# A two-layer gated cross-attention network: a new order of units in each attention's opening and in its rows, and the second attention's code without a loop

## The chip, the cores and the metric

One core of a Trainium2 chip runs the whole network in one launch. The metric is the time of that launch on the device in microseconds (us), less is better. Times come from three runs; the trace comes from one further execution that the hardware profiler recorded.

## The reference

`x` is 8 rows of 224 x 512, the context 8 rows of 750 x 512, both float32. Layer 0 has 16 heads of 32 and an unmasked softmax, layer 1 has 8 heads of 64 and a mask. Four stages follow one another, each gated by a tanh:

```python
x = x + jnp.tanh(g_xattn[0]) * _L0_xattn_ref(_layernorm(x, axis=-1), ctx_1024, ctx_1024, Wq, Wk, Wv, Wo)
x = x + jnp.tanh(g_ffn[0]) * _L0_ffn_ref(_layernorm(x, axis=-1), w1, conv_w, conv_b, w2)
x = x + jnp.tanh(g_xattn[1]) * _L1_xattn_ref(_layernorm(x, axis=-1), ctx_1024, mask, Wq, Wkv, Wo)
x = x + jnp.tanh(g_ffn[1]) * _L1_ffn_ref(_layernorm(x, axis=-1), w_gate, w_up, w_down)
...
    attn = jnp.einsum('bhnd,bhmd->bhnm', q, k) * SCALE        # attention: q from x, k and v from the context
    attn = jax.nn.softmax(jnp.where(mask[:, None, :, :], attn, -jnp.inf), axis=-1)
    out = jnp.einsum('bhnm,bhmd->bhnd', attn, v)
    return out.transpose(0, 2, 1, 3).reshape(B, N, C) @ Wo
```

The first feed-forward block quantises its weights to -1, 0, 1 and has a depthwise convolution; the second rounds activations and weights to FP4 in blocks of 16.

## The kernel before

The stages run one behind another and share the names of their buffers (`a_` is an attention, `f_` a feed-forward block). Both attentions are one function, called twice; `stacked` is true for the first alone. Float32 values are carried as a bfloat16 high part and a low part: ScalarE writes the high part ("hi"), VectorE the low one by a subtraction ("lo"), so each product is three TensorE matmuls.

**The opening (`prologue`).** SyncE loads the weights, ScalarE and VectorE split them (L672, L822), and VectorE normalises row 0 (L855) with roots that GpSimd worked out (`row_roots`, L603). TensorE first waits for all four split weights. Then come the units of row 0: X transposes the normalised row (L1113), K, Q and V project (L1069), M transposes the maxima that scale the softmax (L1109). After each K and Q unit SyncE regroups the result through memory into the score operand (L443, L453), one after another. Between these, the two halves of the scores of each head (L1161) have their maxima taken on VectorE (L933; with a mask L928).

**The rows (`quarter`, `walk`).** The other work is cut into quarters of a row: quarters 2 and 3 of row b, then 0 and 1 of row b+1. For each of its heads a quarter does the transposed scores of row b (L1141; with masks L1138), exponent and high part on ScalarE (L751, L761), low part on GpSimd (L637, three instructions), the product with V on TensorE (L1179), and in the same slots the scores and maxima of row b+1. `quarter_units` says which units of the next rows go into a quarter and `slots_of` into which slot of which head. Two banks take the units' results in turn, so a unit that is late holds up what follows on TensorE, whose order is fixed by the code.

**What the second attention has besides.** From its 24 quarters in the loop each also rounds a piece of the last block's weights: `weight_step` on VectorE takes the scales (L945 to L948), multiplies by their inverse (L951) and takes powers (L1884, L1885); GpSimd rounds (`round_weights`, L652, L1894). The unit M(1) of the next row, which needs the row's last maximum, stands at the end of quarter 3 (`last_unit`). VectorE and GpSimd run a loop over two rows at a time for the first six rows of both attentions; TensorE's code is written out in the first and such a loop in the second.

**The last block** opens with ScalarE's tanh of the gate and VectorE's low parts of the weights (L2212).

## Time and profile before

| | |
|---|---|
| median of 3 runs | 2384.8 us (2383.3 to 2389.01) |
| profiled execution | 2391.48 us, span of its trace 2389.7 us |
| mean granted TensorE clock | 0.917 |
| busy share of the span | PE 84%, PE loads 59%, VectorE 63%, ScalarE 40%, GpSimd 51% |
| costliest group | L1179, PE, 4608 matmuls, 194.4 us busy |

Shares are means over four stages that differ. In the trace the first attention ends at about 825 us, the first feed-forward block at 1170, the second attention at 1989, and the last block with the span. "PEclk" is the TensorE clock that was granted, as a share of 2.4 GHz: 0.50 is the lower of its two levels. In brackets behind a row of a timeline stand the idle time of the engine ahead of it and what ended it.

### The profile page before, as it was taken

What the parts mean: (1) busy time and instruction counts of PE and PEld (TensorE: products, weight loads), DVE (VectorE), ACT (ScalarE), POOL (GpSimd) and SP (SyncE); (2) the same over time, 40 slices, a digit from 0 to 9 for tenths busy, and PEclk for the clock granted to TensorE, in tenths of its full rate; (3) what the DMA queues carried; (4) which work ended last, traced back from release to release, by engine and by line L of the source; (5) the groups of instructions that cost most, each with busy time, mean ns of one, the idle gap of its engine ahead of it and who ended that gap; (6) DMA issues with size and microseconds to landing.
All of it is one profiled execution on the core that took longest, in us unless ns stands there. A gap on an engine that the chain in (4) does not pass through costs nothing. (4 is left out here: it accounts for less than half of the span.)

```text
span 2389.7 us, 43091 instructions
## 1 busy us (share of the span) xinstructions
PE 2006.7 (84%) x15208; PEld 1407.2 (59%) x15208; DVE 1503.2 (63%) x2860; ACT 951.2 (40%) x1289; POOL 1213.0 (51%) x1436
## 2 busy tenths in 40 slices
PE   3678998998998579999378898898988986799997
PEld 2456666666666367778245566666665674455553
DVE  3636666666664279887433566666666645789873
ACT  2146656656657573333113333333333352111111
POOL 4037666667657553323211454555554552577763
PEclk8989999999997589999688899999999997899998
DMA  5243443443431231100432344334434342010100
GB/s 173 63 118 92 119 113 95 113 113 96 112 92 34 80 113 32 46 27 28 134 108 80 90 116 134 107 107 129 120 104 120 103 142 70 18 36 31 35 22 31
DMA packets 184026, 208.83 MB, mean 87 GB/s; under 512 B 61480, under 2 KB 145704, under 8 KB 183336
## 3 DMA queue, kind: packets, MB, share of 16 engines
q1 hardware_dynamic: 183848, 206.46, 31.0%
q8 instruction: 112, 1.84, 0.3%
q14 instruction: 66, 0.54, 0.1%
HBM read 138.61 MB, written 67.53 MB: 86 GB/s over the span
## 5 line engine op out<-in xcount | busy, mean ns | idle before, releaser
L637 POOL TENSOR_TENSOR a_p_hl<-a_p,a_p_hl 125x448 bf16<-125x448 f32 x576 | 619.5, 1077 | 689.9 <-ACT a_p_hl L761 659.5
L751 ACT ACTIVATE a_p<-a_psum 125x1344 f32<-125x1344 f32 x192 | 247.8, 1290 | 147.7 <-PE a_psum L1141 140.1
L761 ACT ACTIVATE a_p_hl<-a_p 125x1344 bf16<-125x1344 f32 x192 | 254.0, 1323 | 115.3 <-PE a_psum L1179 112.2
L933 DVE TENSOR_REDUCE a_nm<-a_psum 112x1 f32<-112x750 f32 x256 | 236.0, 929 | 32.9 <-PE a_psum L1161 31.1
L1179 PEld LDWEIGHTS a_psum<-a_v_st,a_p_hl 125*128 125x128 bf16 x4608 | 182.9, 100 | 45.4 <-issue 22.6
L1179 PE MATMUL a_psum<-a_v_st,a_p_hl 125*128 125x65 bf16 (+2 forms) x4608 | 194.4, 197 | 13.9 <-POOL a_p_hl L637 11.6
L1161 PE MATMUL a_psum<-a_k_st,a_q_st 96*112 96x375 bf16 x512 | 136.7, 354 | 75.5 <-DVE a_nm L933 64.8
L1807 PE MATMUL f_conv<-f_u,f_taps 128*128 128x224 f32 x768 | 161.2, 359 | 22.1 <-DVE f_u L1659 21.3
L898 DVE TENSOR_TENSOR a_v_st<-a_psum,a_v_st 125x512 bf16<-125x512 f32 x96 | 66.3, 691 | 160.2 <-ACT a_v_st L729 160.2
L892 DVE TENSOR_TENSOR a_k_tmp<-a_psum,a_k_tmp 128x375 bf16<-128x375 f32 x128 | 69.0, 546 | 151.6 <-ACT a_k_tmp L722 146.6
L1807 PEld LDWEIGHTS f_conv<-f_u,f_taps 128*128 128x128 f32 x768 | 141.6, 191 | 31.6 <-DVE f_u L1659 26.9
L1069 PE MATMUL a_psum<-a_chl,a_w 128*128 128x375 bf16 x768 | 143.7, 341 | 7.0 <-DVE a_chl L864 6.1
L1069 PE MATMUL a_psum<-a_chl,kept_w 128*128 128x375 bf16 x768 | 147.0, 349 | 1.0 <-DVE a_xnT L903 0.7
L729 ACT ACTIVATE a_v_st<-a_psum 125x512 bf16<-125x512 f32 x96 | 58.4, 608 | 216.1 <-PE a_psum L1069 216.1
L1161 PE MATMUL a_psum<-kept_k,a_q_st 128*112 128x375 bf16 (+1 forms) x512 | 124.2, 343 | 17.7 <-DVE a_nm L928 11.9
L722 ACT ACTIVATE a_k_tmp<-a_psum 128x375 bf16<-128x375 f32 x128 | 61.6, 484 | 194.5 <-PE a_psum L1069 173.6
L928 DVE CUSTOM_DVE_ANT_0 a_psum<-a_psum,a_mask_b 112x750 f32<-112x750 f32 x128 | 120.1, 944 | 23.4 <-PE a_psum L1161 17.1
L1069 PE MATMUL a_psum<-a_w,a_chl 128*125 128x512 bf16 x576 | 133.2, 381 | 0.9 <-DVE a_xnT L903 0.9
L1069 PE MATMUL a_psum<-kept_w,a_chl 128*125 128x512 bf16 x576 | 133.5, 381 | 0.0
L2132 POOL TENSOR_TENSOR f_ht<-f_ht,f_hp 128x512 f32<-128x512 f32 (+1 forms) x84 | 99.0, 1207 | 61.0 <-DVE f_hp L1885 59.9
L1141 PE MATMUL a_psum<-a_q_st,kept_k 128*125 128x224 bf16 (+1 forms) x768 | 128.7, 275 | 0.0
L1538 ACT ACTIVATE f_t<-f_conv,f_cb 128x224 f32<-128x224 f32 x128 | 57.5, 449 | 166.6 <-PE f_conv L1807 166.6
(251 smaller groups left out, 4030.2 us busy)
## 6 DMA issues: line engine op xcount, KB each, us to landing
a_k<-a_k_tmp SPq DMA_DIRECT2D x64, 375.0 KB, 3.0
a_k_st<-a_k SPq DMA_DIRECT2D x96, 187.5 KB, 3.4
kept_k<-a_k SPq DMA_DIRECT2D x96, 187.5 KB, 3.4
a_c<-in_ctx_t SPq DMA_DIRECT2D x16, 750.0 KB, 5.5
ctx_parts<-a_chl SPq DMA_DIRECT2D x16, 750.0 KB, 9.8
a_chl<-ctx_parts SPq DMA_DIRECT2D x16, 750.0 KB, 6.9
a_q_st<-a_q SPq DMA_DIRECT2D x192, 56.0 KB, 2.2
rounded<-a_fw SPq DMA_DIRECT2D x24, 352.0 KB, 3.7
```

Of the source, the lines that this page charges most:

```text
L637: ins = nc.gpsimd.tensor_tensor(p_hl[0:MC, h % 2, 1, cols], p32[0:MC, h % 2, cols], p_hl[0:MC, h % 2, 0, cols], ALU.subtract)
L751: nc.scalar.activation(p32[0:MC, par, :].rearrange("p (b n) -> p b n", b=3), st[0:MC, :, 0:2 * S], ACT.Exp, scale=scale).then_inc(exp_done, 1)
L761: nc.scalar.activation(p_hl[0:MC, par, 0, :], p32[0:MC, par, :], ACT.Copy).then_inc(phi_done, 1)
L892: ins = nc.vector.tensor_tensor(k_tmp[:, cc % 2, 1, cols], bank[:, 0:MK], k_tmp[:, cc % 2, 0, cols], ALU.subtract)
L928: ins = nc.vector.tensor_tensor_reduce(out=sm_[0:HALF, 0:2, 0:MK], in0=sm_[0:HALF, 0:2, 0:MK], in1=mask_b[:, b.parity, s, :].rearrange("p ...
L933: ins = nc.vector.tensor_reduce(out, sm_[0:HALF, 0:2, 0:MK], AX.XY, ALU.max, negate=True)
L1069: ins = nc.tensor.matmul(out, lhs, rhs, start=(c == 0 and n == 0), stop=(c == KC - 1 and n == 2))
L1141: ins = nc.tensor.matmul(out, k_stack(b.parity, at(h), rows)[:, j * MC:(j + 1) * MC], q_stack(b.parity, at(h), rows), start=(t == 0 and no ...
L1161: ins = nc.tensor.matmul(sm_[0:HALF, kh, 0:MK], q_stack(b.parity, at(h), rows)[:, s * HALF:(s + 1) * HALF], k_stack(b.parity, at(h), rows) ...
L1179: ins = nc.tensor.matmul(ob[:, c0:c0 + width], p_hl[0:MC, h % 2, part, j * S + Q0[s]:j * S + Q0[s] + P], v_st[0:MC, b.parity, j, h, 0:widt ...
L1807: ins = nc.tensor.matmul(conv[:, g % 2, c * S:(c + 1) * S], taps[:, g * GC + c, k, :], u[:, g % 2, c, k:k + S], start=(k == 0), stop=(k == 2))
L2132: ins = nc.gpsimd.tensor_tensor(ht[:, cols], ht[:, cols], hp[:, cols], op)
```

## The change

1. Opening of both attentions: `prologue_steps` is a new list in which the splits of context (C) and weights (W) are steps among the units; weights come in the order K, Q, V, O and TensorE waits for each as it needs it; three V units stand among the K and Q units, and the units of row 1 among the heads. SyncE's loads of the next context move accordingly. GpSimd works out the roots of row 1 ahead of its memset of ones, which is cut into 16 (8) pieces.
2. Rows of the second attention: M(1) moves from the end of quarter 3 to the second place of quarter 0; each half of the next row is normalised ahead of the powers of the weight step; the product moves from VectorE to GpSimd (`scale_weights`).
3. In the last row of both attentions the low parts of odd heads are VectorE's (`low_part`).
4. The second attention's code has no loop on TensorE and VectorE. TensorE has 6482 rows of code in place of 5273, VectorE 2024 in place of 1777.
5. Last block: the first low part goes ahead of the normalisation, the gate's tanh behind the first high part.

The core of the diff; semaphores, renamed helpers and the same reordering on the other engines are left out:

```diff
-        if q == 0 and b.exists() and b.number != 0 and stacked:
+        if q == 0 and b.exists() and b.number != 0:
...
-    def last_unit(q, b):
-        return [("M", 1, b + 1)] if q == 3 and (b + 1).exists() and not stacked else []
...
-            at = [0, 1, 3, 6, 7][5 - len(units):]
+            at = [0, 1, 2, 3, 6, 7] if len(units) == 6 else [0, 1, 3, 6, 7][5 - len(units):]
...
-        steps = [("X", 0, b), ("X", 1, b)]
-        for cc in range(KC):
-            steps += [("K", (cc, 0), b), ("K", (cc, 1), b), ("Q", cc, b)]
+        nb = b + 1
+        steps = [("C", 0, b), ("W", 0, b), ("W", 1, b), ("K", (0, 0), b), ("X", 0, b), ("X", 1, b), ("W", 2, b),
+                 ("K", (1, 0), b), ("Q", 0, b), ("C", 1, b), ("K", (0, 1), b), ("W", 3, b), ("Q", 1, b),
+                 ("K", (1, 1), b), ("V", 0, b), ("V", 1, b), ("K", (2, 0), b), ("K", (2, 1), b), ("Q", 2, b),
+                 ("V", 2, b), ("K", (3, 0), b), ("K", (3, 1), b), ("Q", 3, b), ("C", 0, nb)]
+        if stacked:
+            behind = {1: [("V", 3, b)], 2: [("K", (0, 0), nb)], 3: [("V", 4, b)], 5: [("V", 5, b), ("C", 1, nb)],
+                      7: [("X", 0, nb)], 8: [("X", 1, nb)], 9: [("M", 0, b)], 10: [("K", (0, 1), nb)],
+                      12: [("Q", 0, nb)]}
+        else:
+            behind = {0: [("V", 3, b)], 1: [("V", 4, b)], 2: [("V", 5, b), ("C", 1, nb)], 3: [("K", (0, 0), nb)],
+                      4: [("X", 0, nb)], 5: [("X", 1, nb), ("M", 0, b)], 6: [("K", (0, 1), nb)], 7: [("Q", 0, nb)]}
         for h in range(H):
-            steps += [("heads", h, b)]
-            steps += [("V", j, b) for j in range(NJ) if j * H // NJ == h]
-            if h in (H2, H2 + 1):
-                steps += [("X", h - H2, b + 1)]
-            if h == H2 + 1:
-                steps += [("M", 0, b)]
-        return steps + [("M", 1, b), ("K", (0, 0), b + 1), ("K", (0, 1), b + 1), ("Q", 0, b + 1)]
+            steps += [("heads", h, b)] + behind.get(h, [])
+        return steps + [("M", 1, b)]
...
                     quarter(q, b + 1)
...
+        W_ORDER = (1, 0, 2, 3)
+        W_NEEDED = {"K": 1, "Q": 2, "V": 3}
...
+        def low_by_vector(b, h):
+            return b.number == B - 1 and h % 2 == 1
...
-                if stacked:
-                    load_ctx(b + 1, 0)
...
-                    if stacked and step == ("M", 1, b):
-                        load_ctx(b + 1, 1)
...
+                    if step[0] == "C":
+                        if stacked and step == ("C", 0, b + 1):
+                            load_ctx(b + 1, 1)
...
+                    if step == ("K", (0, 1), b + 1):
+                        sp.wait_ge(w_hi, 4)
+                        sp.wait_ge(w_lo, 4)
...
-                    if not stacked and step[0] == "V" and step[1] in (NJ // 2 - 1, NJ - 1):
+                    if stacked and step == ("K", (0, 1), b):
+                        load_ctx(b + 1, 0)
+                    if not stacked and step in (("Q", KC - 1, b), ("V", NJ - 1, b)):
...
-                        load_ctx(b + 1, step[1] * 2 // NJ)
+                        load_ctx(b + 1, 0 if step[0] == "Q" else 1)
...
-            sp.wait_ge(w_hi, 4)
-            sp.wait_ge(w_lo, 4)
+            sp.wait_ge(w_hi, 2)
+            sp.wait_ge(w_lo, 2)
...
+            row_roots(Item(1, 1, 1))
...
+            pool.wait_ge(roots, 2)
...
-            ones = k_st[m_row:m_row + 3, :, 0:16 * M] if stacked else k_st[m_row:m_row + 3, :, 8 * M:16 * M]
-            nc.gpsimd.memset(ones, 1.0).then_inc(preset, 1)
+            for par in range(2):
+                for c0 in range(0 if stacked else 8 * M, 16 * M, 2 * M):
+                    ins = nc.gpsimd.memset(k_st[m_row:m_row + 3, par, c0:c0 + 2 * M], 1.0)
+                    if (par, c0) != (1, 14 * M):
+                        chain.link(ins)
+            ins.then_inc(preset, 1)
...
-                row_roots(b + 1)
...
+                        if fp4_weights and b.number is None and h == q * HC + 1:
+                            scale_weights(q, b)
+                        if low_by_vector(b, h):
+                            continue
...
+            def scale_weights(q, b):
+                pool.wait_ge(f_inverse, b.index * 4 + q - 1)
+                pool.wait_ge(f_rounded, b.index * 4 + q - 1)
+                for n, cols in enumerate(halves):
+                    ins = fp4_rescale(nc.gpsimd, ft[:, cols], fw[:, q % 2, cols],
+                                      f_small[:, cols.start // 16:cols.stop // 16])
+                    if n == 0:
+                        chain.link(ins)
+                ins.then_inc(f_product, 1)
...
-                if not fp4_weights or b.number is not None:
+                if not fp4_weights or b.number is not None and not 0 <= 4 * b.number + q - 2 < FP4_PIECES:
...
-                step = at - 1 if q == 2 else at
-                if step == 0:
+                if at == 1:
                     dve.wait_ge(fw_in[par], (b.index * 2 + (q - 2) // 2 + 1) * 16)
...
-                if step == 1:
-                    dve.wait_ge(f_rounded, b.index * 4 + q - 1)
-                    link(nc.vector.tensor_tensor(in_blocks(ft[:, :]), in_blocks(w), f_small[:, :].unsqueeze(
-                        2).broadcast_to(blocks), ALU.mult))
-                if step == 2:
+                    nc.vector.tensor_scalar(f_small[:, :], f_small[:, :], 1.0 - 2.0 ** -22, None,
+                                            ALU.mult).then_inc(f_inverse, 1)
+                if at == 3:
+                    dve.wait_ge(f_product, b.index * 4 + q - 1)
                     fp4_powers(link, w, ft[:, :]).then_inc(f_scaled, 1)
...
+            def low_part(b, h):
+                hd = b.index * H + h
+                dve.wait_ge(phi_done, hd + 1)
+                dve.wait_ge(pv_done, hd - 1)
+                nc.vector.tensor_tensor(p_hl[0:MC, h % 2, 1, :], p32[0:MC, h % 2, :], p_hl[0:MC, h % 2, 0, :],
+                                        ALU.subtract).then_inc(plo_vector, 1)
...
-                normalise(b)
-                split_ctx(b, 0)
-                split_weights()
-                split_ctx(b, 1)
-                dve.wait_ge(gate_ready, 1)
...
-                    if step == ("K", (0, 0), b):
+                    if step == ("W", 1, b):
+                        normalise(b)
+                    if step == ("Q", 1, b):
                         row_moments(b + 1)
+                    if step == ("V", 2, b):
...
-                    weight_step(q, b, 2 * j)
...
+                    next_context(2 * j + 1)
...
-                    next_context(2 * j + 1)
...
-            NORMALISED = {(2, 5): [0], (2, 7): [1]} if stacked else {(2, 3): [0, 1]}
+            NORMALISED = {(2, 5): [0], (2, 7): [1]} if stacked else {(2, 2): [0], (2, 3): [1]}
...
-            walk(dve.Fori, quarter, prologue, enter, leave)
+            LINKS = LINKS_PER_ROW + (4 * 4 if fp4_weights else 0)
+            walk(dve.Fori, quarter, prologue, enter, leave, PAIRS if stacked else 0)
...
-            pe.wait_ge(w_lo, 4)
...
+                    elif step[0] not in ("C", "W"):
+                        if step[0] in W_NEEDED:
+                            pe.wait_ge(w_lo, W_NEEDED[step[0]])
                         unit_products(step)
+                pe.wait_ge(w_lo, 4)
...
-                for unit in last_unit(q, b):
-                    unit_products(unit)
...
-            walk(pe.Fori, quarter, prologue, units.enter_loop, units.leave_loop, 0 if stacked else PAIRS)
+            walk(pe.Fori, quarter, prologue, units.enter_loop, units.leave_loop, 0)
...
+                if n == 0:
+                    act.wait_ge(g_in, 16)
+                    nc.scalar.activation(tg[:, :], g_sb[:, :], ACT.Tanh).then_inc(gate_ready, 1)
...
+            w_lo(0)
             x_normalise(0)
-            dve.wait_ge(gate_ready, 1)
...
-            for n in range(2 * NG):
+            for n in range(1, 2 * NG):
...
-                if n == 0:
+                if n == 1:
...
+            dve.wait_ge(gate_ready, 1)
```

What the change does to the order of instructions is shown at three places. TensorE at the start of the first attention, before (`a_chl` is the split context, `a_xnT` the transposed row, `a_w` the weights, `a_ident` the identity):

```order
L1113 MATMUL a_psum<-a_ident,a_xn 128x112 x8
L1069 MATMUL a_psum<-a_chl,a_w 128x375 x24
L1069 MATMUL a_psum<-a_xnT,a_w 128x224 x12
L1069 MATMUL a_psum<-a_chl,a_w 128x375 x24
L1069 MATMUL a_psum<-a_xnT,a_w 128x224 x12
L1069 MATMUL a_psum<-a_chl,a_w 128x375 x24
L1069 MATMUL a_psum<-a_xnT,a_w 128x224 x12
L1069 MATMUL a_psum<-a_chl,a_w 128x375 x24
L1069 MATMUL a_psum<-a_xnT,a_w 128x224 x12
L1161 MATMUL a_psum<-a_k_st,a_q_st 112x375 x4
```

and now:

```order
L1117 MATMUL a_psum<-a_chl,a_w 128x375 x12
L1161 MATMUL a_psum<-a_ident,a_xn 128x112 x8
L1117 MATMUL a_psum<-a_chl,a_w 128x375 x12
L1117 MATMUL a_psum<-a_xnT,a_w 128x224 x12
L1117 MATMUL a_psum<-a_chl,a_w 128x375 x12
L1117 MATMUL a_psum<-a_xnT,a_w 128x224 x12
L1117 MATMUL a_psum<-a_chl,a_w 128x375 x12
L1117 MATMUL a_psum<-a_w,a_chl 125x512 x24
L1117 MATMUL a_psum<-a_chl,a_w 128x375 x24
L1117 MATMUL a_psum<-a_xnT,a_w 128x224 x12
L1117 MATMUL a_psum<-a_w,a_chl 125x512 x12
L1117 MATMUL a_psum<-a_chl,a_w 128x375 x24
```

One K unit of 12 products now stands ahead of the transposition of the row, and V units (`a_w,a_chl`) stand ahead of the last K and Q units, where they stood among the heads.

VectorE in the looped rows of the second attention, second head of quarter 2, before (`a_ft` and `a_fw` are the weight piece, `a_nm` the maxima, `a_xn` the normalised row, `a_v_st` the value operand):

```order
L951 TENSOR_TENSOR a_ft<-a_fw,a_f_small 128x704
L43 REGISTER_ALU
L919 REGISTER_ALU
L927 MEMSET a_carrier 128x1
L928 ISA a_psum,a_nm<-a_psum,a_mask_b 112x2x375
L928 ISA a_nm 112x1
L1884 TENSOR_SCALAR a_fw<-a_ft 128x704
L43 REGISTER_ALU
L1885 TENSOR_SCALAR a_fw<-a_fw 128x704
L847 TENSOR_SCALAR a_xn<-a_xin,a_mv,a_root 112x512 x2
```

and now:

```order
L893 TENSOR_SCALAR a_xn<-a_xin,a_mv,a_root 112x512
L1009 COPY a_o_lo<-a_psum 128x128
L1010 RECIPROCAL a_o_rec<-a_psum 128x2
L1011 TENSOR_TENSOR a_psum<-a_psum,a_o_lo 128x2x64
L1013 TENSOR_TENSOR a_o<-a_psum,a_o_rec 128x2x64
L942 TENSOR_TENSOR a_v_st<-a_psum,a_v_st 125x8x64
L972 ISA a_psum,a_nm<-a_psum,a_mask_b 112x2x375
L972 ISA a_nm 112x1
L893 TENSOR_SCALAR a_xn<-a_xin,a_mv,a_root 112x512
L1933 TENSOR_SCALAR a_fw<-a_ft 128x704
L1934 TENSOR_SCALAR a_fw<-a_fw 128x704
```

The product L951 is gone from this engine, and the two halves of the row (L847 before, L893 now) stand ahead of the powers, the first one also ahead of the outputs of the last heads.

TensorE at the seam of quarter 3 and quarter 0 in the second attention, before (`a_nm` marks the unit M, `kept_k` the keys, REGISTER_ALU and the bare ISA are the loop's address arithmetic):

```order
L1069 MATMUL a_psum<-a_xnT,kept_w 128x224 x12
L1155 REGISTER_ALU
L1161 MATMUL a_psum<-kept_k,a_q_st 112x375 x4
L1090 ISA
L1096 REGISTER_ALU
L1109 MATMUL a_psum<-a_ident,a_nm 4x112 x2
L1096 REGISTER_ALU
L1069 MATMUL a_psum<-a_chl,kept_w 128x375 x12
L1129 REGISTER_ALU
L1131 ISA
L1138 MATMUL a_psum<-a_maskT_b,a_ident_b 125x224
L1141 MATMUL a_psum<-a_q_st,kept_k 125x224 x2
```

and now:

```order
L1117 MATMUL a_psum<-a_xnT,kept_w 128x224 x12
L1209 MATMUL a_psum<-kept_k,a_q_st 112x375 x4
L1117 MATMUL a_psum<-a_chl,kept_w 128x375 x12
L1186 MATMUL a_psum<-a_maskT_b,a_ident_b 125x224
L1189 MATMUL a_psum<-a_q_st,kept_k 125x224 x2
L1186 MATMUL a_psum<-a_maskT_b,a_ident_b 125x224
L1189 MATMUL a_psum<-a_q_st,kept_k 125x224 x2
...
L1186 MATMUL a_psum<-a_maskT_b,a_ident_b 125x224
L1189 MATMUL a_psum<-a_q_st,kept_k 125x224 x2
L1157 MATMUL a_psum<-a_ident,a_nm 4x112 x2
L1209 MATMUL a_psum<-kept_k,a_q_st 112x375 x4
```

The M unit, which stood right behind the four score matmuls whose maximum it needs, now follows a K unit and a whole head's six pairs of transposed scores, of which the "..." hides three. The address arithmetic is gone.

## Rows read from the trace of the kernel before

**Rows 1.** Four stretches of the span: busy time, instructions, granted clock, transfers.

```profile
core 0: us, PE busy (x) PEld busy (x) DVE busy (x) ACT busy (x) POOL busy (x), PEclk, DMA share, GB/s
0.00:131.00 131.00, 67.03 (x338) 40.19 (x339) 62.98 (x84) 27.37 (x37) 27.07 (x33) 0.88 0.43 119
155.00:751.00 596.00, 536.34 (x5403) 400.16 (x5402) 385.20 (x723) 371.86 (x387) 388.39 (x395) 0.95 0.42 103
1170.00:1276.00 106.00, 67.56 (x337) 38.59 (x338) 44.48 (x80) 23.01 (x34) 16.72 (x30) 0.77 0.47 138
1351.00:1919.00 568.00, 506.29 (x3947) 357.82 (x3948) 360.25 (x848) 206.60 (x251) 289.56 (x340) 0.94 0.39 114
```

**Rows 2.** Timeline of all engines, first attention's opening; columns: start, us, engine.

```profile
13.42 6.69 DVE L822 TENSOR_TENSOR a_w<-a_k_st,a_w 128x2048 bf16<-128x2048 f32 x3
...
22.84 1.73 PE L1113 MATMUL a_psum<-a_ident,a_xn 112*128 112x112 f32 x8 [22.84 <-DVE a_w L822]
22.89 20.09 POOL L614 MEMSET a_k_st<- 3x24000 bf16 x1 [12.05 <-DVE a_w L822]
...
46.41 1.00 DVE L855 TENSOR_SCALAR a_xn<-a_xin,a_mv,a_root 112x512 f32<-112x512 f32 x2 [16.64 <-POOL a_root L603]
...
47.93 2.42 PE L1069 MATMUL a_psum<-a_xnT,a_w 128*128 128x224 bf16 x12 [16.30 <-DVE a_k_tmp L892]
```

**Rows 3.** Timeline of SyncE's queue, same opening, first and last of eight regroups.

```profile
48.35 0.38 SPq L443 DMA_DIRECT2D a_k<-a_k_tmp  x1
...
84.89 1.25 SPq L453 DMA_DIRECT2D a_q_st<-a_q  x3
```

**Rows 4.** Timeline of TensorE, start of the first attention's quarters.

```profile
141.23 0.87 PE L1161 MATMUL a_psum<-a_k_st,a_q_st 96*112 96x375 bf16 x2 [7.84 <-DMA a_q_st<-a_q]
```

**Rows 5.** Timeline of all engines, second attention's opening.

```profile
1182.66 2.29 DVE L822 TENSOR_TENSOR kept_w<-kept_k,kept_w 128x2048 bf16<-128x2048 f32 x1 [1.38 <-ACT kept_w L672]
...
1193.22 1.73 PE L1113 MATMUL a_psum<-a_ident,a_xn 112*128 112x112 f32 x8 [26.70 <-DVE kept_w L822]
...
1208.65 2.42 PE L1069 MATMUL a_psum<-a_xnT,kept_w 128*128 128x224 bf16 x12 [6.45 <-DVE a_k_tmp L892]
...
1287.51 1.67 PE L1161 MATMUL a_psum<-kept_k,a_q_st 128*112 128x375 bf16 x4 [5.88 <-DMA a_q_st<-a_q]
```

**Rows 6.** TensorE's waits, second attention's six looped rows: waited for, us, times, longest.

```profile
PE a_psum L1113 <- DVE a_xn L847: 29.2, 6, 4.9
PE a_psum L1109 <- DVE a_nm L928: 21.3, 12, 3.3
PE a_psum L1161 <- DVE a_nm L928: 10.8, 17, 1.1
```

**Rows 7.** Timeline of TensorE and VectorE, second attention, around quarter boundaries.

```profile
1540.15 1.68 DVE L951 TENSOR_TENSOR a_ft<-a_fw,a_f_small 128x704 f32<-128x704 f32 x1
...
1544.55 1.00 PE L1113 MATMUL a_psum<-a_ident,a_xn 112*128 112x112 f32 x4 [4.91 <-DVE a_xn L847]
...
1566.18 0.53 PE L1109 MATMUL a_psum<-a_ident,a_nm 112*4 112x112 f32 x2 [3.31 <-DVE a_nm L928]
```

**Rows 8.** Stretches as in Rows 1, the two slow-clock ones of one row.

```profile
1542.20:1549.00 6.80, 4.45 (x24) 4.45 (x25) 3.89 (x7) 0.59 (x2) 4.64 (x5) 0.50 0.62 181
...
1566.00:1569.50 3.50, 3.32 (x12) 1.71 (x13) 1.19 (x4) 0.35 (x1) 3.26 (x5) 0.52 0.37 129
```

**Rows 9.** TensorE's waits, first attention's quarters, then its weight loads' waits.

```profile
PE a_psum L1161 <- DVE a_nm L933: 54.6, 80, 2.3
...
PEld a_psum L1069 <- issue: 4.2, 26, 0.2
```

**Rows 10.** Timeline of GpSimd, the end of the first attention.

```profile
778.58 28.97 POOL L637 TENSOR_TENSOR a_p_hl<-a_p,a_p_hl 125x448 bf16<-125x448 f32 x27 [0.60 <-ACT a_p_hl L761]
```

**Rows 11.** The page's costliest groups: ScalarE's high parts.

```profile
L761 ACT ACTIVATE a_p_hl<-a_p 125x1344 bf16<-125x1344 f32 x192 | 254.0, 1323 | 115.3 <-PE a_psum L1179 112.2
```

**Rows 12.** Timeline of VectorE, opening of the last feed-forward block.

```profile
1997.69 1.87 DVE L2212 TENSOR_TENSOR f_gu<-f_gp,f_gu 128x512 bf16<-128x512 f32 x3
```

More of the change, by code:

```diff
@@ L131, in quarter_units @@
             else:
-                units += chunk[:1] + maxima + chunk[1:] if stacked else maxima + chunk
+                units += chunk[:1] + maxima + chunk[1:] if stacked or q == 0 else maxima + chunk
         if (b + 1).exists():
@@ L284, in cross_attention @@
         mid = Item(3, 1)
-        UBODY = sum(len(quarter_units(q, b) + last_unit(q, b)) for q, b in ((2, mid), (3, mid), (0, mid + 1), (1, mid + 1)))
+        UBODY = sum(len(quarter_units(q, b)) for q, b in ((2, mid), (3, mid), (0, mid + 1), (1, mid + 1)))
         PAIRS = (B - 2) // 2
@@ L538, in quarter @@
                     load_residual(b + -1)
-                for unit in quarter_units(q, b) + last_unit(q, b):
+                for unit in quarter_units(q, b):
                     n = after_unit(unit)
@@ L643, in quarter @@
                     round_weights(q, b)
+            halves = [slice(n * FP4_COLS // 2, (n + 1) * FP4_COLS // 2) for n in range(2)] if fp4_weights else []
+            def scale_weights(q, b):
[7 more added lines that the diff above has]
+                ins.then_inc(f_product, 1)
             def round_weights(q, b):
@@ L648, in round_weights @@
                 pool.wait_ge(f_scaled, b.index * 4 + q - 1)
-                halves = [slice(n * FP4_COLS // 2, (n + 1) * FP4_COLS // 2) for n in range(2)]
                 for op in (ALU.add, ALU.subtract):
@@ L708, in unit_hi_part @@
                 kind, k, b = unit
-                if unit[:2] == ("K", (0, 0)) and (b.number == 1 or not stacked and b.number != 0):
-                    split_ctx(b, 1, None)
                 n = units.next()
@@ L805, in quarter @@
                     mask_bias(b + 2)
-                for unit in last_unit(q, b):
-                    unit_hi_part(unit)
             walk(act.Fori, quarter, prologue, units.enter_loop, units.leave_loop)
@@ L877, in unit_lo_part @@
                 kind, k, b = unit
-                if unit[:2] == ("K", (0, 0)) and (b.number == 1 or not stacked and b.number != 0):
-                    split_ctx(b, 1)
                 n = units.next()
```

90 lines of the change are left out of this document (48 added, 42 removed).

## The prediction

> **What bounds the kernel now.** I read the stretches of the span first [rows 1]. In the 596 us of the first attention's written-out rows TensorE is busy for 536, at a clock of 0.95; in the 568 us of the second one's looped rows for 506, at 0.94, with VectorE at 360 and GpSimd at 290. Neither of these is near full, so TensorE and what it waits for set the time. The two openings are another matter: TensorE is busy for only 67 of 131 us and for 68 of 106 us. So I read the timelines of both openings, and TensorE's waits in the rows.
>
> In the first opening TensorE does nothing for 22.84 us, until the fourth weight is split [rows 2]. GpSimd then starts a memset of 20.09 us, and the roots of row 1 stand behind it; VectorE's normalisation waits 16.64 us for them, and because K's low part stands behind that normalisation, TensorE waits 16.30 us. SyncE then regroups K and Q units one by one from 48.35 to 84.89 [rows 3], and at 141.23 TensorE waits 7.84 us for a regroup [rows 4]. The second opening has the same pattern in small [rows 5]: a start at 1193.22 although the first weight is split at 1182.66 + 2.29 = 1184.95, 6.45 us behind the root, 5.88 us behind a regroup.
>
> In the second attention's six looped rows the list of TensorE's waits has two that come back in each row [rows 6]: the normalised row ahead of unit X (29.2 us, six times, at most 4.9) and the maxima ahead of unit M (21.3 us, 12 times for two units a row, at most 3.3, so nearly all of it M(1)'s). At the seam the reason is seen [rows 7]: VectorE multiplies a weight piece for 1.68 us and only later normalises, and X waits 4.91 us; M(1) waits 3.31. Behind each of the two the granted clock is 0.50 and 0.52, for 6.8 and 3.5 us, in which TensorE is busy for 4.45 and 3.32 [rows 8]. A row takes about 568 / 6 = 95 us.
>
> **The change, part by part.** *First opening.* TensorE's first K unit needs the context's split and one weight. VectorE begins its weights at 13.42, the normalisation of row 0 (two halves in 1.00) is moved behind the first, which takes 6.69 / 3 = 2.23: 13.42 - 1.0 + 2.2 = 14.6, 8.2 us earlier [rows 2]. The wait of 16.3 is removed, since the roots of row 1 are worked out before the memset and the normalisation waits for no large piece. What GpSimd has left, the memset in 16 pieces, still needs 20 us, but its user is the score operand's M rows and the quarters, far later; if it were late, its 20 us would be seen once, ahead of quarter 0. The stall of 7.8 goes, as row 1's Q(0) is done four heads ahead of the end rather than last. From 22.84 to 131 there are 108.2 us, of which 67.0 busy and 16.3 that wait: 24.9 of other idle time, mostly K and Q units in lockstep with ScalarE, VectorE and SyncE. V units between them fill some; I take a third, 8. Together 8.2 + 16.3 + 7.8 + 8 = **40.3** (bounds 28, if the lockstep stays and a third of the wait comes back, and 48, if two thirds of the idle time fill).
>
> *Second opening.* 1193.22 - 1184.95 = 8.3; the root's 6.45; the regroup's 5.9; of the other idle time (1276 - 1193.2 - 67.6 - 6.45 = 8.8) some 5. Together **25.6** (bounds 16 and 32) [rows 1, 5].
>
> *Six rows.* The first half of the row is now normalised one maximum ahead, the second ahead of the powers and without the product of 1.68 in front. So X's 4.9 goes. M(1) stands behind a K unit and a head's scores: its 3.3 goes [rows 6, 7]. The work that ran at half clock, 4.45 + 3.32 = 7.8 us, takes half as long at the full one: 3.9 [rows 8]. Against it stand new waits: with the two gone TensorE arrives sooner at scores whose bank waits for a maximum. The second attention pays 10.8 us for that in its six rows, 1.8 each [rows 6]; the first, which runs without the two stalls, pays 54.6 in 596 us, which is 54.6 x 95 / 596 = 8.7 for each 95 us [rows 1, 9]. The excess is at most 6.9; I take 2.3, a third, as VectorE is less busy here (63% against 65%) and loses the product. So 4.9 + 3.3 + 3.9 - 2.3 = 9.8 a row, times six **59** (bounds 6 x (12.1 - 6.9) = 31 and 6 x 12.1 = 73). A seventh M(1), in row 6 behind the loop, gives 3.3 + 3.3 / 2 = **5**.
>
> The product on GpSimd is costed at nothing: that engine is idle for half of the 568 us [rows 1]. It stands ahead of an odd head's low part, so uncovered it would put off TensorE's value products by its own length, 24 times one or two microseconds.
>
> *Written-out code* is costed at nothing on TensorE: in the first attention, written out, it gets through 5403 matmuls in 596 us, 9.1 a microsecond, and its weight loads wait for issue 4.2 us in all [rows 1, 9]; the second has 3947 in 568, 6.9 a microsecond.
>
> *Last rows.* GpSimd's low part sets the first attention's end: 27 instructions in a run of 28.97 us, three a head, 3.22 each for nine heads [rows 10]. ScalarE has a high part of 1.32 a head [rows 11] and an exponent over the same 1344 columns, taken at the same, and becomes the bound at 2.6: 0.6 less for seven heads or so is **4**; in the second attention, where maxima and outputs are lighter, I take **2** (both together 0 to 10). VectorE's low part of 1344 columns is estimated as 2.23 x 1344 / 2048 = 1.5 us from the weights' splits.
>
> *Last block.* Four low parts of weights (three in 1.87, [rows 12]) move into VectorE's idle time ahead of the normalisation: **2.5** (0 to 4).
>
> **Sum.** 40.3 + 25.6 + 59 + 5 + 6 + 2.5 = 138.4. Against the profiled execution's own 2391.5 this is 2253.1; the median of the runs lies 6.7 lower, so 2246.
>
> **The rivals.** *B, the maxima take over.* VectorE's maxima stand behind TensorE's earlier scores and each row wins only half. For it: the first attention's 54.6 us [rows 9]. Against: the second one's 10.8. Half of 64 lost: 2246 + 32 = 2278.
>
> *C, the regroups set the openings.* SyncE's eight regroups take 36.5 / 8 = 4.6 us each [rows 3]; V units don't shorten that chain, which only starts sooner. Then half of 66 is lost: 2279. Against: the roots' waits lie within that chain and lengthen it.
>
> *D, VectorE's and GpSimd's subtractions hold each other up.* The one product in Rows 7 takes 1.68 us while GpSimd is at its low parts. In the last rows the low parts of twelve odd heads (eight and four) on VectorE would meet GpSimd's of the even ones; each twice as long is 12 x 1.5 = 18, half of it on the path, and the gain of 6 is gone: 2246 + 9 + 6 = 2261. The Trainium skill says this on its page "SBUF — State Buffer", section "Who interferes with whom": VectorE's second pair of ports is GpSimd's, and it is an exclusive lock. By that rule an instruction of VectorE with two inputs in SBUF waits for GpSimd's to end, or GpSimd for it; the trace's 1.68 us agrees with it.
>
> *E, slower: the written-out code starves TensorE.* It decides from 139 + 7 us over six rows, 24 us a row. A row has 3947 x 95 / 568 = 660 matmuls and as many loads, so each of 1320 instructions would have to cost 18 ns more. Against it stands the first attention, whose written-out code already issues faster and waits 4.2 us [rows 9]. It would give 2395.
>
> *F, the change does nothing*: every stall removed is replaced in full by the next, 2385. Little speaks for it, since two of the removed stalls are ahead of any work.
>
> **How the numbers follow.** The sum, 0.55 (its own range 2225 to 2270); B 0.13; C 0.12; D 0.08; E 0.03; F 0.01; and 0.08 that more is won than the sum has, as its idle times in the openings (17 and 4 us not counted) and other shares of half clock go too, 2215. B and C together would give 2311 and are left outside. The range 2215 to 2290 holds about 0.8. Within 0.3% is what a measurement of this kernel can't tell from no change, 7 us: faster by more 0.96, within 0.01, slower 0.03.
>
> **What would show it.** In the trace after: TensorE's first matmul at about 14.6 and its second attention's at 1185 less what was won before; the 16 memsets behind both rows' roots; TensorE with no wait over 3 us for a normalised row; the first opening shorter by 32 or more; rows of the second attention of about 85 us instead of 95; no wait at unit M(1) and clock 0.9 or more in both places; waits for maxima there of 2 to 8 us a row (over that it is B); loads' waits for issue under 10 us in all (over 100 is E); GpSimd's low parts in the last rows 1.03 us each as before (over 1.3 is D). The prediction is wrong if the time that the stalls free comes back at the next wait in the same fixed order, on ScalarE or in the regroups, which I have only sampled.

## The result, and the profile after

| | before | changed | ratio, 95% interval |
|---|---|---|---|
| median | 2386.8 us (4 runs) | 2280.7 us (2278.6 to 2286.6, 4 runs) | 0.9561 [0.9538, 0.9583] |
| profiled execution | 2391.5, span 2389.7 | 2280.4, span 2278.6 | |
| granted clock | 0.917 | 0.937 | |

106 us are won where 138 were forecast. To see where, both traces are cut at the same head: ScalarE writes one high part for each head, so the n-th row of that line is the same work in both. From the timeline of ScalarE before, the high parts of the first head and of the first head of quarter 1 in the first attention, of its last head, of the second attention's first head, of the first and of the one past the last head of its six looped rows, and of its last head:

```profile
134.75 1.32 ACT L761 ACTIVATE a_p_hl<-a_p 125x1344 bf16<-125x1344 f32 x1
...
166.35 1.32 ACT L761 ACTIVATE a_p_hl<-a_p 125x1344 bf16<-125x1344 f32 x1
...
802.54 1.32 ACT L761 ACTIVATE a_p_hl<-a_p 125x1344 bf16<-125x1344 f32 x1
...
1282.05 1.31 ACT L761 ACTIVATE a_p_hl<-a_p 125x1344 bf16<-125x1344 f32 x1
...
1330.34 1.32 ACT L761 ACTIVATE a_p_hl<-a_p 125x1344 bf16<-125x1344 f32 x1 [1.41 <-PE a_psum L1179]
...
1905.86 1.32 ACT L761 ACTIVATE a_p_hl<-a_p 125x1344 bf16<-125x1344 f32 x1 [1.50 <-PE a_psum L1179]
...
1966.91 1.32 ACT L761 ACTIVATE a_p_hl<-a_p 125x1344 bf16<-125x1344 f32 x1
```

The same seven in the timeline of ScalarE of the changed kernel:

```profile
108.52 1.32 ACT L811 ACTIVATE a_p_hl<-a_p 125x1344 bf16<-125x1344 f32 x1
...
130.12 1.32 ACT L811 ACTIVATE a_p_hl<-a_p 125x1344 bf16<-125x1344 f32 x1
...
761.03 1.32 ACT L811 ACTIVATE a_p_hl<-a_p 125x1344 bf16<-125x1344 f32 x1
...
1223.51 1.31 ACT L811 ACTIVATE a_p_hl<-a_p 125x1344 bf16<-125x1344 f32 x1
...
1266.35 1.32 ACT L811 ACTIVATE a_p_hl<-a_p 125x1344 bf16<-125x1344 f32 x1 [1.41 <-PE a_psum L1227]
...
1797.21 1.32 ACT L811 ACTIVATE a_p_hl<-a_p 125x1344 bf16<-125x1344 f32 x1 [1.50 <-PE a_psum L1227]
...
1858.28 1.32 ACT L811 ACTIVATE a_p_hl<-a_p 125x1344 bf16<-125x1344 f32 x1
```

| stretch | before | changed | won | forecast |
|---|---|---|---|---|
| start to quarter 1, first attention | 166.35 | 130.12 | 36.2 | 40.3 |
| its rows and its last row | 636.19 | 630.91 | 5.3 | 4 |
| to the second attention's looped rows | 527.80 | 505.32 | 22.5 | 25.6 |
| its six looped rows | 575.52 | 530.86 | 44.7 | 59 |
| its last row, to the last head | 61.05 | 61.07 | 0.0 | 7 |
| the rest of the span | 422.79 | 420.32 | 2.5 | 2.5 |

Together 111.1, the difference of the two spans and 5 more than that of the medians. One trace is one execution: where nothing differs in the code, landmarks lie some us apart (below, at e11). Each of the six rows takes 88.5 us in place of 95.9. The stretch of these rows in the changed kernel, and TensorE's waits in it (waited for, us, times, longest), against [rows 1] and [rows 6]:

```profile
core 0: us, PE busy (x) PEld busy (x) DVE busy (x) ACT busy (x) POOL busy (x), PEclk, DMA share, GB/s
1266.00:1797.00 531.00, 495.92 (x3967) 349.59 (x3965) 320.05 (x751) 206.93 (x252) 328.99 (x402) 0.96 0.42 123
```

```profile
PE a_psum L1209 <- DMA a_q_st<-a_q: 32.3, 13, 4.8
PE a_psum L1209 <- DVE a_nm L972: 1.6, 2, 1.1
```

X's and M's waits of [rows 6] are gone, and waits for maxima are 1.6 us in all where 2 to 8 a row were expected. In their place stands one that [rows 6] doesn't have: 32.3 us for `a_q_st`, the operand that SyncE regroups. The timeline of SyncE and TensorE at one seam of quarter 3 and quarter 0 shows what it is:

```profile
1382.91 0.37 SPq L466 DMA_DIRECT2D a_k<-a_k_tmp  x1
...
1386.06 1.88 SPq L476 DMA_DIRECT2D kept_k<-a_k  x3
...
1387.99 0.59 SPq L511 DMA_DIRECT2D rounded<-a_fw  x1
...
1388.62 0.43 SPq L466 DMA_DIRECT2D a_q<-a_q_tmp  x1
...
1391.04 0.36 PE L1157 MATMUL a_psum<-a_ident,a_nm 112*4 112x112 f32 x2
...
1392.21 1.88 SPq L476 DMA_DIRECT2D a_q_st<-a_q  x3
...
1395.80 1.68 PE L1209 MATMUL a_psum<-kept_k,a_q_st 128*112 128x375 bf16 x4 [4.40 <-DMA a_q_st<-a_q]
```

SyncE sends K out at 1382.91, waits for it to land, issues its three loads at 1386.06, writes back a weight piece, and only at 1388.62 sends Q, whose loads go at 1392.21. TensorE is through M(1) at 1391.4 and stands until 1395.80; its four matmuls then take 1.68 us, at the lower level of the clock.

### The profile page after: what moved, and what is told of

Its sections match the earlier page's. It is cut to its first block and busy times, and to the rows that moved or that the text cites. A ratio compares the mean times of both kernels' runs of the same rounds, so it can differ in the third digit from the quotient of the medians.

```text
span 2278.6 us, 42253 instructions
## 1 busy us (share of the span) xinstructions
PE 1975.2 (87%) x15208; PEld 1385.9 (61%) x15208; DVE 1477.8 (65%) x2752; ACT 949.6 (42%) x1289; POOL 1214.7 (53%) x1470
## 5 line engine op out<-in xcount | busy, mean ns | idle before, releaser
L678 POOL TENSOR_TENSOR a_p_hl<-a_p,a_p_hl 125x448 bf16<-125x448 f32 x540 | 578.7, 1073 | 533.8 <-ACT a_p_hl L811 505.3
L1117 PE MATMUL a_psum<-a_chl,kept_w 128*128 128x375 bf16 x768 | 141.9, 339 | 24.4 <-DVE kept_w L868 18.3
L1117 PE MATMUL a_psum<-a_chl,a_w 128*128 128x375 bf16 x768 | 140.5, 335 | 18.9 <-DVE a_w L868 14.9
L1117 PEld LDWEIGHTS a_psum<-a_chl,kept_w 128*128 128x128 bf16 x768 | 74.7, 102 | 79.4 <-issue 38.8
```

The source lines that it names most:

```text
L678: ins = nc.gpsimd.tensor_tensor(p_hl[0:MC, h % 2, 1, cols], p32[0:MC, h % 2, cols], p_hl[0:MC, h % 2, 0, cols], ALU.subtract)
L1117: ins = nc.tensor.matmul(out, lhs, rhs, start=(c == 0 and n == 0), stop=(c == KC - 1 and n == 2))
```

## The experiments

Each kernel is the changed one but for its edit. The ratio is against the kernel before on the same chip; "against the changed one" is the difference from 0.9561, times 2387 us. A ratio's interval is about 0.002 wide on either side, so 5 us, and what is told of less than some 7 us leans on the traces.

**e1_m1_back.** M(1) stands at the end of quarter 3 again.

```diff
-        if q == 0 and b.exists() and b.number != 0:
+        if q == 0 and b.exists() and b.number != 0 and stacked:
+    def last_unit(q, b):
+        return [("M", 1, b + 1)] if q == 3 and (b + 1).exists() and not stacked else []
```

> The changed kernel with one part undone: in the second attention the unit M(1) stands again at the end of quarter 3. Theory (the regroup hides behind it): in the changed kernel's trace TensorE's scores at the start of quarter 0 wait 3.8 to 4.8 us a row for the regroup of unit Q, which stands at the end of quarter 3. With M(1) back, its wait of about 3.3 us returns and runs beside that same regroup, so the wait for the regroup falls by about as much: 0 to 2 us a row, 2281 to 2293. Rival (the prediction's own sum, waits add up): M(1)'s 3.3 and its half clock 1.7 come on top, 5 us in each of seven rows, 2316.

Measured: 0.9478 [0.9461, 0.9495], 20 us *faster* than the changed kernel. Both theories had the wrong sign. TensorE's waits in its six rows:

```profile
PE a_psum L1216 <- DMA a_q_st<-a_q: 15.8, 13, 2.4
PE a_psum L1164 <- DVE a_nm L977: 6.8, 6, 1.1
```

M(1) now waits only 1.1 us, and the regroup 15.8 in place of 32.3. With M(1) at the end of quarter 3, quarter 0's second K unit (2.1 us of matmuls) comes ahead of the scores that need the regroup; in the changed order M(1), 0.36 us long, has that slot and the K unit stands behind the stalled scores. So the move took away a wait of 1 us and uncovered one of 4, with a slow clock behind it: TensorE's work in the six rows is 487 us here, 496 in the changed kernel.

**e2_norm_back.** Both halves are normalised behind the powers again.

```diff
-            NORMALISED = ... else {(2, 2): [0], (2, 3): [1]}
+            NORMALISED = ... else {(2, 3): [0, 1]}
-                    next_context(2 * j + 1)
                     weight_step(q, b, 2 * j + 1)
+                    next_context(2 * j + 1)
```

> The changed kernel with one part undone: in the second attention both halves of the next row are normalised behind the powers of the weight step again. Theory: X's wait comes back, less the product of 1.7 us that is now GpSimd's, so 3 to 4 us a row, and with it a stretch at half clock of some 2 us; Q's regroup at the end of the same quarter is later by as much and takes nothing back. 5 us in each of six rows, 2311 (2299 to 2321). Rival (the slack at the seam takes it): under 1 us a row, within 6 us of the changed kernel's 2281.

Measured: 0.9651 [0.9631, 0.9671], 21 us slower. X's wait is back beside the regroup's, the theory's mechanism, at two thirds of its price (21 us for 30); the regroup's wait is 6 us less than in the changed kernel and gives a part back. TensorE's waits in the six rows:

```profile
PE a_psum L1212 <- DMA a_q_st<-a_q: 26.2, 7, 4.6
PE a_psum L1164 <- DVE a_xn L893: 17.7, 6, 3.0
```

**e3_looped.** The loop on TensorE and VectorE is back in the second attention.

```diff
-            walk(dve.Fori, ..., PAIRS if stacked else 0)
+            walk(dve.Fori, ..., PAIRS)
-            walk(pe.Fori, ..., 0)
+            walk(pe.Fori, ..., 0 if stacked else PAIRS)
```

> The changed kernel with the second attention's first six rows as a loop again on TensorE and VectorE. Theory: written-out code is worth nothing or a microsecond a row (address arithmetic on an engine that waits elsewhere), 2281 to 2290. Rival one: the loop's arithmetic stands in the chain that ends in the regroups, 2 us or more a row, 2293 or more. Rival two (the prediction's case E in small): the written-out code costs supply, and the loop is faster, under 2275.

Measured: 0.9590 [0.9566, 0.9614], 7 us slower, at the limit of what can be told. In the traces a row takes 89.6 us in place of 88.5, so the loop costs about 1 us a row, and there is no sign that the written-out code is short of instructions: it isn't the slower one.

**e4_q3_early.** K and Q of quarter 3 stand earlier.

```diff
+        if not stacked and q == 3 and len(units) == 5:
+            at = [0, 1, 2, 3, 4]
```

> The changed kernel with the units K and Q of quarter 3 in the second attention each one slot or two earlier (slots 2, 3, 4 in place of 3, 4, 6). Theory: the seam's wait for Q's regroup, 3.8 to 4.8 us a row, is due to Q standing last; with it half a head (some 5 us) earlier the wait goes, and the half clock behind it: 4 to 6 us in each of six rows, less if X's units then wait. 2250 (2245 to 2262). Rival: SyncE's queue, which is behind K's regroup and a weight piece, or the K units' wait for the context, sets it; then at most 1 us a row is won, 2275 to 2285.

Measured: 0.9559 [0.9541, 0.9578], nothing won. The timeline of one seam, TensorE's Q unit, SyncE's K loads, its sending of Q, its Q loads, and the scores:

```profile
1381.99 1.31 PE L1119 MATMUL a_psum<-a_xnT,kept_w 128*128 128x224 bf16 x12
...
1386.45 1.88 SPq L478 DMA_DIRECT2D kept_k<-a_k  x3
...
1389.01 0.43 SPq L468 DMA_DIRECT2D a_q<-a_q_tmp  x1
...
1392.46 1.88 SPq L478 DMA_DIRECT2D a_q_st<-a_q  x3
...
1396.05 0.98 PE L1211 MATMUL a_psum<-kept_k,a_q_st 128*112 128x375 bf16 x4 [4.13 <-DMA a_q_st<-a_q]
```

Q's products are done at 1383.3, 3.3 us earlier, and SyncE sends Q no earlier than before, 1389.01: it is still at K. K itself goes out no earlier either (1383.40), since its second unit now waits 0.83 us for the context. Where Q stands was not the cause, as the rival had it.

**e7_pipelined.** e4's slots, and SyncE sends Q before it waits for K; `fill` holds the wait and the three loads that stood in `regroup`.

```diff
     def regroup(...):
         sp.dma_start(dram[cc]..., tmp[...]).then_inc(sent, 16)
+        return lambda: fill(...)
...
     K: held.append(regroup(...)); if not hold: held.pop()()
     Q: held.append(regroup(...)); while held: held.pop(0)()
...
-                    n = after_unit(unit)
+                    n = after_unit(unit, not stacked and q == 3)
```

> The changed kernel with the earlier slots of e4_q3_early and, in quarter 3 of the second attention, SyncE's two regroups side by side: Q's first transfer is sent before SyncE waits for K's. In e4_q3_early Q was ready some 4 us earlier and its transfer left SyncE no earlier, behind K's regroup. Theory: SyncE's serial regroups hold the seam; now the operand lands 3 to 4 us earlier, the wait falls from 4 to 5 us to about 1 and the half clock behind it goes: 3 to 5 us in each of six rows, 2255 to 2267. Rival (the transfers' own time, two of some 2.5 us in a row, or the stall moves on): 2275 or more.

Measured: 0.9423 [0.9401, 0.9445], 33 us faster than the changed kernel and than e4, from which only SyncE's order differs, and a little more than the theory had. One seam in SyncE's and TensorE's timeline:

```profile
1384.93 0.37 SPq L468 DMA_DIRECT2D a_k<-a_k_tmp  x1
...
1385.86 0.53 SPq L468 DMA_DIRECT2D a_q<-a_q_tmp  x1
...
1388.00 1.89 SPq L482 DMA_DIRECT2D kept_k<-a_k  x3
...
1390.05 1.87 SPq L482 DMA_DIRECT2D a_q_st<-a_q  x3
...
1393.75 0.98 PE L1221 MATMUL a_psum<-kept_k,a_q_st 128*112 128x375 bf16 x4 [0.41 <-DMA a_q_st<-a_q]
```

The stretch of its six rows:

```profile
1275.00:1775.00 500.00, 486.10 (x3962) 344.77 (x3961) 318.77 (x753) 207.60 (x252) 329.89 (x402) 0.99 0.45 131
```

Q leaves SyncE 0.9 us behind K, and its loads follow K's with no wait between. TensorE waits 0.41 where it waited 4.40 (4.13 in e4), and the six rows run at a clock of 0.99 in place of 0.96: 83.3 us a row. SyncE's serial queue is the cause of the new wait.

**e8_m1_pipelined.** e7 and e1 together.

> e7_pipelined and M(1) at the end of quarter 3 as in e1_m1_back, which was 20 us faster than the changed kernel with 2.6 us a row left of the wait for the regroup. Theory: both together leave M(1)'s wait of about 1 us a row and none for the regroup: 2250 to 2260 (1 to 2.5 us a row under e1_m1_back). Rival (with the seam's work back ahead of the regroup nothing is left to win): as e1_m1_back, 2261 to 2266.

Measured: 0.9425 [0.94, 0.9449], as e7. Once the regroup is in time, where M(1) stands is worth nothing either way; the 20 us of e1 were all the regroup's.

**e5_product_vector.** The product on VectorE, ahead of the powers.

```diff
+                    link(nc.vector.tensor_tensor(in_blocks(ft[:, :]), in_blocks(w), f_small..., ALU.mult))
...
-                        if fp4_weights and b.number is None and h == q * HC + 1:
-                            scale_weights(q, b)
```

> The changed kernel with the weight piece's product back on VectorE, ahead of the powers and behind the normalised halves. Theory: VectorE has the room, since its order there no longer puts the product ahead of anything that TensorE waits for; 0 to 1 us a row, 2281 to 2290. Rival (VectorE's 0.9 to 1.7 us stand ahead of the next maximum, and with it of the maxima M(1) and the bank): 2 us a row, 2293 or more.

Measured: 0.9571 [0.9547, 0.9596], 2 us slower, inside the noise.

**e6_low_gpsimd.** All low parts of the last rows on GpSimd.

```diff
-            return b.number == B - 1 and h % 2 == 1
+            return False
```

> The changed kernel with all low parts of the last rows on GpSimd. Theory: it costs what the traces of before and after show between the last heads, 4 to 5 us in the first attention, 0 to 1 in the second: 2285 to 2287. Rival (ports are shared and the split gains nothing): 2281, within 1 us.

Measured: 0.9580 [0.9558, 0.9603], 5 us slower, at the limit of what can be told; in its trace the last twenty heads of the first attention take 63.3 us in place of 60.8, and the last sixteen, its last row, 49.1 in place of 46.6. The kernel before took 49.1 too, so VectorE's low parts are worth 2.5 us there.

**e9_roots_late.** The roots of row 1 stand behind the memset.

```diff
-            row_roots(Item(1, 1, 1))
-            pool.wait_ge(roots, 2)
...
             ins.then_inc(preset, 1)
+            pool.wait_ge(preset, 3)
+            row_roots(Item(1, 1, 1))
```

> The changed kernel with the roots of row 1 behind the memset of ones again, in both attentions. Theory: the memset starts at about 35 us in the first attention, when the last weight is split, and takes 20; the roots are ready near 58 instead of 40, VectorE's normalisation, which the changed order places near 45, waits for them and TensorE behind it: 10 to 15 us there, 0 to 5 in the second attention, where the memset is half as long: 2291 to 2301. Rival (the regroups of SyncE set the opening and hide the roots, case C of the prediction): within 4 us of the changed kernel, 2277 to 2285.

Measured: 0.9597 [0.9575, 0.9618], 9 us slower. The timeline of its first opening: the memset, VectorE's normalisation and the K unit behind it:

```profile
36.06 22.36 POOL L646 MEMSET a_k_st<- 3x1500 bf16 x16 [23.86 <-DVE a_w L867]
...
61.88 1.00 DVE L900 TENSOR_SCALAR a_xn<-a_xin,a_mv,a_root 112x512 f32<-112x512 f32 x2 [11.07 <-POOL a_root L635]
...
63.62 3.53 PE L1116 MATMUL a_psum<-a_chl,a_w 128*128 128x375 bf16 x12 [8.86 <-DVE a_v_st L941]
```

The roots' wait is back in the first opening, 8.86 us in place of the 16.30 of [rows 2] (the releaser named is V's low part, which stands behind the normalisation on VectorE), and the units that now stand ahead of it may cover the rest. The first head's high part is at 120.1, later than in any other trace of the new opening. The regroups don't hide the roots, against case C.

**e10_rows_old.** The edits of e1, e2 and e5 together.

> The changed kernel with the second attention's rows in the old order: M(1) at the end of quarter 3, both halves normalised behind the powers, product on VectorE (the three edits of e1, e2 and e5 together). What is left of the change is the openings, the last rows, the last block and the written-out code. Theory: landmarks of the two traces give these 36 + 22 + 5 + 2.5 = 66, and e3_looped says 6 for the written-out code: 2387 - 72 = 2315, 2307 to 2323. So the order of the rows would be worth some 34. Rival (the edits are not additive: with M(1) back and its 20 us the rest of the row order is worth 50 or more): over 2325, or, if M(1) back recovers most by itself, under 2300.

Measured: 0.9594 [0.9569, 0.9618], 8 us slower, and not the 34 that were expected. That is under 2300, as the rival had it, but not because the edits fail to add up: -20, +21 and +2 give +3, which is within the noise of 8. What was missing for the 34 was a fourth edit. TensorE's waits in its six rows have X's back, and M(1)'s is 1.1 us, not 3.3:

```profile
PE a_psum L1172 <- DVE a_xn L896: 23.3, 6, 3.9
PE a_psum L1220 <- DMA a_q_st<-a_q: 7.0, 8, 2.1
PE a_psum L1168 <- DVE a_nm L975: 6.8, 6, 1.1
```

**e12_steps_old.** e10, and the weight step (scales, product, powers) at its old places on VectorE.

```diff
-                if at == 1:
+                step = at - 1 if q == 2 else at
+                if step == 0:
...
+                if step == 1:
+                    link(nc.vector.tensor_tensor(in_blocks(ft[:, :]), ...))
-                if at == 3:
+                if step == 2:
                     fp4_powers(link, w, ft[:, :]).then_inc(f_scaled, 1)
```

> e10_rows_old with one more part of the row order undone: the weight step stands at its old places on VectorE again, scales ahead of a head's second maximum and powers ahead of the last one of the quarter, whose transposition is M(1). e10_rows_old came out at 2296 where 2315 was expected: a row takes 90.5 us in its trace, against 95.9 before, though M(1), the normalisation and the product stand as before, and M(1)'s wait is 1.1 instead of 3.3. Theory (the places of the weight step are a fourth edit that the working of the prediction passed over): M(1)'s wait is again over 3 us, with a stretch at half clock behind it, 3 to 4 us in each of six rows: 2310 to 2322. Rival (the code without a loop is worth more in the old order of the rows than the 6 us of e3_looped): e12 stays within 5 us of e10_rows_old, 2291 to 2301.

Measured: 0.9703 [0.968, 0.9726], 26 us slower than e10 and 34 slower than the changed kernel. M(1)'s wait is back at 3.2:

```profile
PE a_psum L1175 <- DVE a_xn L896: 27.8, 6, 4.7
PE a_psum L1171 <- DVE a_nm L975: 19.8, 9, 3.2
```

So the weight step's places are worth 4.3 us a row (26 by six). In the old ones the powers of quarter 3 stand on VectorE between the last scores and the maximum that M(1) needs; behind the change they follow that maximum. X's wait and the maxima's have a part in the 26 too (23.3 to 27.8 us, and 2.3 to 7.4).

**e11_pipelined_all.** e7, with K and Q sent side by side wherever Q follows K directly, in the quarters of both attentions and, for two of the four pairs, in each opening.

```diff
-                for unit in quarter_units(q, b):
-                    n = after_unit(unit, not stacked and q == 3)
+                todo = quarter_units(q, b)
+                for k, unit in enumerate(todo):
+                    n = after_unit(unit, k + 1 < len(todo) and todo[k + 1][0] == "Q")
```

> e7_pipelined with SyncE's regroups of K and Q side by side wherever Q follows K's second half directly, in both attentions and in the openings. Theory: outside the seam at quarter 0 only 1 us a row waits for a regroup, in the openings 3 us in one place that this edit doesn't reach: 2246 to 2254. Rival one (case C, the regroups set the openings): 5 us or more below e7_pipelined's 2249 to 2252, so under 2244. Rival two (K's operand comes later where Q stands far behind, and new waits arise): 2256 or more.

Measured: 0.9342 [0.9315, 0.9369], 52 us faster than the changed kernel and the fastest of all. The stretch of its six rows:

```profile
1268.00:1756.00 488.00, 481.34 (x3969) 342.82 (x3966) 319.06 (x751) 207.61 (x252) 329.61 (x402) 1.00 0.47 134
```

And the one wait of TensorE that the trace lists there:

```profile
PE a_psum L1223 <- DMA a_q_st<-a_q: 6.7, 6, 2.3
```

A row takes 81.3 us, 2 less than in e7. What went are mostly waits of 0.9 to 2.5 us ahead of quarter 3, which the theory put at 1 us a row, without the slower clock behind them: the regroup's waits fall from 12.5 to 6.7 us, and TensorE's work in the six rows from 486 to 481. That is 12 of the 19 us between e7 and e11. In the first attention's rows nothing is won (630.8 us from quarter 1 to the last head, 630.9 in the changed kernel).

The first opening isn't shorter: its first head's high part is at 113.9, and in the eleven traces with the same opening and the serial queue it lies between 106.8 and 115.1. The second one is: from TensorE's first unit to the first head it takes 76.8 us, and 79.5 to 82.8 in all twelve traces with the serial queue there. The changed kernel's timeline of SyncE and TensorE there shows one wait that has to do with it:

```profile
1195.01 0.60 SPq L403 DMA_DIRECT2D a_chl<-ctx_parts  x1
...
1200.42 3.92 PE L1117 MATMUL a_psum<-a_chl,kept_w 128*128 128x375 bf16 x12 [3.71 <-issue]
```

SyncE sends the first half of row 1's context only behind the last regroup. It lands 5.3 us later, at 1200.3, and the first K unit of row 1, which reads it, starts at 1200.42 after a wait of 3.71 us for which the profile names no releaser. All twelve traces have this wait, of 2.9 to 5.8 us; e11, where the load leaves SyncE 4.7 us earlier in the opening, doesn't. So case C is wrong in the first opening and, as far as one trace of e11 can show it, right for some 4 us in the second.

## Why the prediction came out as it did

The direction and the order of size were right: 106 us won against 138. By its own steps:

- **First opening**, 40.3 forecast, 36.2 found, and the traces with this opening differ by up to 8 us among themselves. TensorE's first product is at 14.9 (14.6 was worked out), the wait for the roots and the stall at quarter 0 are gone, and the memset, 22.7 us long now, hid behind other work. Of the "other idle time, a third" the opening's own waits took some back. TensorE's waits up to 150 us (us, times, longest):

```profile
PE a_psum L1209 <- DVE a_nm L977: 16.1, 18, 3.7
PE a_psum L1117 <- DVE a_w L868: 14.9, 1, 14.9
PE a_psum L1117 <- DVE a_chl L910: 4.0, 1, 4.0
PE a_psum L1117 <- DVE a_q_tmp L939: 3.1, 1, 3.1
```

  The 16.1 us of maxima (13.8 of them up to quarter 1, where there were 10.2 before) and the two waits of 4.0 and 3.1 for the second half of the context and the Q unit's low part are what is left. e9 puts the roots' part at 9.
- **Second opening**, 25.6 forecast, 22.5 found. The regroup's stall didn't go, as "5.9" had it, but shrank to 3.3 us, and the wait of 3.7 for row 1's context is new (e11).
- **Six rows**, "9.8 a row, times six 59": 44.7 found, and of the four terms two were wrong. *X, 4.9 and its clock*: right in mechanism, e2 gives 3.5 a row where some 7 were counted for wait and clock. *M(1), 3.3 and its clock*: the move was the failing step. e1 shows that it cost 3.3 us a row (20 by six). What took M(1)'s wait down from 3.3 to 1.1 was the weight step's new place on VectorE, which my working passed over; e10 and e12 price it at 4.3 a row. *New waits, 2.3*: these were sought at the maxima (case B), where 0.3 a row came; they came at SyncE's regroup, 5.4 a row, which I had seen as the stall of a quarter's start in both openings [rows 4, 5] and not followed into the rows, where X's and M(1)'s waits had hidden it. *The product*: at nothing, as e5 says. *The written-out code at nothing*: about 1 us a row, e3. So part of the 44.7 isn't the order's.
- **The seventh M(1) and the second attention's last row**, 7 forecast, nothing found. The forecast took row 6's M(1) to wait as in the looped rows; row 6 has no weight step, and M(1)'s wait there was 1.2 us before and is 1.2 after. The low parts on VectorE are worth nothing there (61.05 and 61.07).
- **First attention's last row**, 4 forecast; the row alone 2.5 (e6), with the rows ahead of it 5.3. Right within what can be told.
- **Last block**, 2.5 forecast and 2.5 found in the two traces, for the whole rest of the span; no run took it apart, so its cause is not shown.
- **The rivals.** B didn't come. C: e9 and e11 speak against it in the first opening, where TensorE waits for no regroup; it holds for some 4 us in the second, and SyncE's queue cost most in the rows, where C didn't look. E: e3 speaks against it. D: the two engines do hold each other up (below), but by 0.36 us for a low part in the mean and not by its whole length, and the last rows still came out even or faster.

The openings, the last rows, the last block and the code without a loop make 71 of the 105 us (e12), the new order of the rows 34. That the total comes so near is partly luck: the forecast gave M(1)'s move 5 us a row, the move cost 3.3, and the weight step's new place, which the forecast didn't have, gave 4.3.

## What to carry to other kernels

Before a wait is removed, look for the transfers that run beside it: the next wait in the same fixed order is often one that the first had hidden, and it needs its own price, from the issuing engine's queue, not from the transfer's duration. An issuing queue that waits for each transfer to land before it sends the next serialises independent transfers; sending both and then waiting was worth 33 us at one seam and 52 everywhere, as much as the whole new order of the rows or more. And a short unit that is moved out of a slot gives the slot to another: what stands ahead of the stalled work matters as much as what was taken away.

## What the runs showed of the hardware

VectorE and GpSimd hold each other up. Of VectorE's twelve low parts in the last rows five meet no instruction of GpSimd and take 1.56 us each (the estimate was 1.5); seven begin while one is under way and take 1.81 to 2.18. One of each kind, in the changed kernel's timeline of the first attention's last row:

```profile
738.88 1.56 DVE L1002 TENSOR_TENSOR a_p_hl<-a_p,a_p_hl 125x1344 bf16<-125x1344 f32 x1 [0.86 <-ACT a_p_hl L811]
...
741.45 3.26 POOL L678 TENSOR_TENSOR a_p_hl<-a_p,a_p_hl 125x448 bf16<-125x448 f32 x3 [3.13 <-ACT a_p_hl L811]
...
743.94 2.18 DVE L1002 TENSOR_TENSOR a_p_hl<-a_p,a_p_hl 125x1344 bf16<-125x1344 f32 x1 [1.20 <-ACT a_p_hl L811]
```

GpSimd's three instructions, 1.03 each as before, end at 744.71, which is 0.77 us into VectorE's; that one takes 0.62 longer than alone. In all seven GpSimd's runs on for 0.40 to 0.77 us, and VectorE takes 0.25 to 0.62 longer: the engine that comes second waits for nearly all of what the first has left. It holds the other way round too: in e5 a low part of GpSimd that begins while VectorE's product is under way takes 1.56 us in place of 1.03. And the two instructions that normalise row 1 take 3.26 us together while GpSimd's memset runs (at 50.21 in the changed kernel), and 1.00 behind it in e9. The Trainium skill's page "SBUF — State Buffer", section "Who interferes with whom", has an exclusive lock between the two; the trace agrees, with the 0.62 us above. In the last rows it was too little to decide anything.

A single stall of 4 us costs more than itself: the granted clock is 0.65 over the 9 us around the seam of the changed kernel (1391 to 1400), and 0.99 over e7's six rows, where no stall is longer than 2.5 us. Shorter ones aren't free either: with twelve regroup waits of up to 2.5 us in e7 and six of up to 2.3 in e11, TensorE's work in the six rows is 486 us and 481.
